# Routing logits of a mixture-of-experts layer: tokens stationary, gate weights moving

## The reference

```python
x = x + ffn(cond(x))                       # h = cond(x), [8192, 512]
logits = h @ gate_w.T                      # [8192, 64]
scores = softmax(logits, axis=-1)
topk_w, topk_i = top_k(scores, 6)          # the 6 experts of a token
# each expert takes its first 64 tokens: buf [64, 64, 512]
y = (silu(buf @ w_gate) * (buf @ w_up)) @ w_down
out = sum of y * topk_w, per token
shared = (silu(h @ sw_gate) * (h @ sw_up)) @ sw_down
```

## Time and profile before

| | us |
|---|---|
| median of three runs | 1214.61 |
| lowest and highest of the three | 1214.23, 1215.86 |
| the profiled execution | 1215.23 |
| its span, first to last instruction | 1213.4 |

### The profile page before, as it was taken

The page is one execution under the profiler, slowest core; times in us unless marked ns, Lnnn a source line. Parts: engine busy times, 40 slices in busy tenths (PEclk is TensorE's granted clock), DMA queues, the critical chain, the costliest instruction groups (busy, mean ns, idle before and its releaser), DMA issues.

```text
span 1213.4 us, 15977 instructions
## 1 busy us (share of the span) xinstructions
PE 1207.8 (100%) x5764; PEld 893.9 (74%) x5764; DVE 856.0 (71%) x1852; ACT 331.7 (27%) x630; POOL 269.7 (22%) x246
## 2 busy tenths in 40 slices
PE   9999999999999999999999999999999999999998
PEld 8888888888888888888866666666666666666666
DVE  6998989989889888886656556555655564655652
ACT  4544243433423443244111111120111201111111
POOL 0000000000000000000135355263453553553431
PEclk9999999999999999999999999999999999999999
DMA  9857445372543725245767988988989989999863
GB/s 200 211 137 195 96 122 130 83 172 67 165 106 84 184 73 153 61 135 189 249 218 248 334 267 274 349 273 277 342 235 335 314 280 305 295 306 301 275 147 84
DMA packets 159968, 250.92 MB, mean 207 GB/s; under 512 B 23633, under 2 KB 94673, under 8 KB 158737
## 3 DMA queue, kind: packets, MB, share of 16 engines
q1 hardware_dynamic: 143968, 223.53, 58.5%
q0 software_dynamic: 14048, 25.18, 10.5%
q10 hardware_dynamic: 1872, 1.18, 0.3%
HBM read 197.14 MB, written 61.10 MB: 213 GB/s over the span
## 4 chain that ended last, share of the span: by engine, by line
PE 93%; DVE 5%; issue 1%; ACT 0%; DMA 0%; POOL 0%; DVEq 0%; POOLq 0%; ACTq 0%
PE bank L1423 22%; PE bank L1424 22%; PE bank L1425 22%; PE bank L1625 13%; PE bank L1640 7%; PE bank L1456 2%; PE bank L1481 1%; PE bank L1544 1%; PE bank L1543 1%; PE bank L1479 1%; PE bank L1550 1%; PE bank L1492 1%; DVE hl L887 0%; DMA hg<-table,idx_quarter 0%; DVE x L902 0%
## 5 line engine op out<-in xcount | busy, mean ns | idle before, releaser
L1423 PE MATMUL bank<-hh,gu 128*128 128x512 f32 x704 | 278.0, 395 | 0.0
L1424 PE MATMUL bank<-hl,gu 128*128 128x512 f32 x704 | 274.2, 390 | 0.0
L1425 PE MATMUL bank<-hh,gu 128*128 128x512 f32 x704 | 274.1, 389 | 0.0
L600 POOL DMA_INDIRECT hg<-table,idx_quarter x128 | 124.7, 974 | 646.6 <-DVE idx_hi L1309 596.6
L1423 PEld LDWEIGHTS bank<-hh,gu 128*128 128x128 f32 x704 | 132.2, 188 | 39.1 <-issue 12.8
L1425 PEld LDWEIGHTS bank<-hh,gu 128*128 128x128 f32 x704 | 132.2, 188 | 27.9
L1424 PEld LDWEIGHTS bank<-hl,gu 128*128 128x128 f32 x704 | 132.3, 188 | 26.2
L668 ACT ACTIVATE ah<-prod 128x512 fp32r<-128x512 f32 x96 | 60.6, 632 | 302.0 <-DVE prod L969 295.9
L1382 DVE STREAM_TRANSPOSE eactT<-eact 32x96 f32<-32x96 f32 (+1 forms) x512 | 133.9, 262 | 7.9
L1423 PE MATMUL bank<-sdh,ah 128*128 128x512 f32 x320 | 126.0, 394 | 0.3 <-issue 0.3
L1424 PE MATMUL bank<-sdl,ah 128*128 128x512 f32 x320 | 124.6, 390 | 0.0
(11 more groups left out here) (126 smaller groups left out, 1676.0 us busy)
## 6 DMA issues: line engine op xcount, KB each, us to landing
wg<-in_L_ffn_w_gate_dram SPq DMA_DIRECT2D x64, 704.0 KB
wu<-in_L_ffn_w_up_dram SPq DMA_DIRECT2D x64, 704.0 KB
wd<-in_L_ffn_w_down_dram SPq DMA_DIRECT2D x64, 512.0 KB
table<-hrow SPq DMA_DIRECT2D x64, 256.0 KB, 4.3
x<-in_x_dram SPq DMA_DIRECT2D x60, 256.0 KB, 6.9
wd<-in_L_ffn_w_down_dram SPq DMA_DIRECT2D x64, 192.0 KB
out_dram<-outst SPq DMA_DIRECT2D x35, 256.0 KB
outst<-in_x_dram SPq DMA_DIRECT2D x32, 256.0 KB, 3.5
```

The lines of the kernel that those rows point to most:

```text
L600: nc.gpsimd.indirect_dma_start(out=hg[p % 3][:, b, :], out_offset=None, in_=quarters, in_offset=bass.IndirectOffsetOnAxis(ap=idx_quarter[: ...
L1423: nc.tensor.matmul(o, st_h, mv_h, start=first_mm, stop=False)
L1424: nc.tensor.matmul(o, st_h, mv_l, start=False, stop=False)
L1425: return nc.tensor.matmul(o, st_l, mv_h, start=False, stop=last_mm)
```

## The change

The logits of a chunk are computed in one step. `logits(n)` now takes the tokens as stationary operand: for each of four pieces of 128 tokens, 4 matmuls with a 128 x 128 piece of hh stationary and the 128 columns of gw2 moving, then 4 with a piece of hl stationary and only the 64 high columns of gw2 moving (the product of the low parts is left out). The result has tokens on partitions at once, in the bank from which `take_low` and `route` read before. `logits_raw`, `take_lraw`, the transposes, the buffer lsb (its bytes stay reserved, so no other buffer moves) and two semaphores go. The new `logits` stands where `logits_raw` stood; nothing stands any longer where the transposes stood. `take_low(b)` moves ahead of `silu(v, 0)` on ACT.

```diff
--- before.py
+++ after.py
@@ -114,7 +114,7 @@
         w3p = keep("w3p", [P, QC, D])
         qb = keep("qb", [P, 2 * B, KC])
         gw2 = keep("gw2", [P, KC, 2 * E], F32R)
-        lsb = keep("lsb", [P, CH])
+        keep.at += 4 * CH
         gu_end = keep.at
         hrow = keep("hrow", [P, CH // SQ, P])
         sc = keep("sc", [P, 2, J, E])
@@ -231,8 +231,6 @@
             hl_ready = sem("hl_ready")
             rows_taken = sem("rows_taken")
             rows_stored = sem("rows_stored")
-            lraw_filled = sem("lraw_filled")
-            lraw_taken = sem("lraw_taken")
             logits_filled = sem("logits_filled")
             llow_ready = sem("llow_ready")
             route_step = sem("route_step")
@@ -348,9 +346,6 @@
         def cond_bank(n, oc):
             return bank[(5, 6, 1, 2)[oc] if n == 0 else (3, 4, 5, 6)[oc] if n == 1 else (4, 5, 6, 4)[oc]]
 
-        def lraw_bank(n):
-            return bank[7 if n == 0 else 5]
-
         def logits_bank(n):
             return bank[7] if n == 0 else bank[3] if n % 2 == 0 else bank[6]
 
@@ -682,17 +677,12 @@
                 if n == 0 and oc == 0:
                     act.wait_ge(bias_loaded[1], 16 * (P // SQ))
                 if oc == 0:
-                    wait(act, s.lraw_filled, n)
+                    wait(act, s.logits_filled, n)
                     wait(act, s.gu_filled, GT * (n // 2))
                 nc.scalar.activation(h32[:, oc, :], cond_bank(n, oc)[:, :], ACT.Relu,
                                      bias=b2c[:, oc:oc + 1]).then_inc(s.cond_taken, 1)
                 act.wait_ge(s.cond_taken, KC * n + oc + 1)
                 copy(hh[:, oc, :], h32[:, oc, :]).then_inc(s.hh_ready, 1)
-
-            def take_lraw(n):
-                act.wait_ge(s.lraw_filled, n + 1)
-                wait(act, s.logits_filled, n)
-                copy(lsb[:, :], lraw_bank(n)[:, :]).then_inc(s.lraw_taken, 1)
 
             def take_low(n):
 
@@ -782,7 +772,6 @@
             split_xm(1, 1)
             split_piece(1)
             split_piece(2)
-            take_lraw(0)
 
             def body(i):
                 a, b, c, d = 2 * i, 2 * i + 1, 2 * i + 2, 2 * i + 3
@@ -796,7 +785,6 @@
                         silu_table()
                 if i == 0:
                     split_piece(3)
-                take_lraw(b)
                 if i == 0:
                     split_piece(4)
                     take_low(a)
@@ -804,9 +792,9 @@
                     split_piece(6)
                 if 0 < i < ND - 1:
                     split_xm(c, 0)
-                silu(v, 0)
                 if i > 0:
                     take_low(b)
+                silu(v, 0)
                 split_a(v, 0)
                 if not more:
                     take_ranks(i)
@@ -848,7 +836,6 @@
                     split_xm(d, 1)
                     if i < 2:
                         take_ranks(i)
-                    take_lraw(c)
 
             for i in range(ND):
                 body(i)
@@ -1429,8 +1416,6 @@
                     pe.wait_ge(s.xmh_ready, halves(n))
                     pe.wait_ge(s.xml_ready, halves(n))
                     pe.wait_ge(s.cond_taken, KC * n)
-                if oc == 1:
-                    pe.wait_ge(s.lraw_taken, n)
                 if oc == 2:
                     pe.wait_ge(s.z_ready, n if n % 2 == 0 else n - 1)
                 if oc == 3:
@@ -1469,28 +1454,27 @@
                 elif n == 1 and oc == KC - 1:
                     op.then_inc(s.cond_begun, 1)
 
-            def logits_raw(n):
-                pe.wait_ge(s.cond_taken, KC * n + 3)
+            def logits(n):
+
+                o = logits_bank(n)
                 if n == 0:
                     pe.wait_ge(s.gw2_ready, 2)
-                o = lraw_bank(n)
-                for k in range(KC):
-                    pe.wait_ge(s.hh_ready, KC * n + k + 1)
-                    nc.tensor.matmul(o[:, :], gw2[:, k, :], hh[:, k, :], start=(k == 0), stop=False)
-                    pe.wait_ge(s.hl_ready, KC * n + k + 1)
-                    op = nc.tensor.matmul(o[:, :], gw2[:, k, :], hl[:, k, :], start=False, stop=(k == KC - 1))
-                op.then_inc(s.lraw_filled, 1)
-
-            def logits(n):
-                pe.wait_ge(s.lraw_taken, n + 1)
-                if n > 0 and n % 2 == 0:
+                elif n % 2 == 0:
                     pe.wait_ge(s.z_ready, n - 1)
                     pe.wait_ge(s.cond_taken, 2 * KC)
-                elif n > 0:
+                else:
                     pe.wait_ge(s.cond_taken, KC * (n + 1))
                 for j in range(J):
-                    op = nc.tensor.transpose(logits_bank(n)[:, j * P:(j + 1) * P], lsb[:, j * P:(j + 1) * P],
-                                             ident[:, :])
+                    t = slice(j * P, (j + 1) * P)
+                    for k in range(KC):
+                        if j == 0:
+                            pe.wait_ge(s.hh_ready, KC * n + k + 1)
+                        nc.tensor.matmul(o[:, j * P:(j + 1) * P], hh[:, k, t], gw2[:, k, :], start=(k == 0), stop=False)
+                    for k in range(KC):
+                        if j == 0:
+                            pe.wait_ge(s.hl_ready, KC * n + k + 1)
+                        op = nc.tensor.matmul(o[:, j * P:j * P + E], hl[:, k, t], gw2[:, k, 0:E], start=False,
+                                              stop=(k == KC - 1))
                 op.then_inc(s.logits_filled, 1)
 
             def gu_tile(v, t):
@@ -1573,7 +1557,7 @@
             op.then_inc(s.gateT_filled, 1)
             for oc in range(KC):
                 cond_half(1, oc, 0)
-            logits_raw(0)
+            logits(0)
             for oc in range(KC):
                 cond_half(1, oc, 1)
 
@@ -1581,18 +1565,12 @@
                 a, b, c, d = 2 * i, 2 * i + 1, 2 * i + 2, 2 * i + 3
                 v, more = i, 2 * i + 2 < NCH
                 if i > 0:
-                    cond_tile(b, 0)
-                    logits(a)
-                    for oc in range(1, KC):
+                    for oc in range(KC):
                         cond_tile(b, oc)
                     down_tile(v - 1, 3)
-                else:
-                    logits(a)
-                logits_raw(b)
+                logits(b)
                 for t in range(GT):
                     gu_tile(v, t)
-                    if t == (2 if i == 0 else 0):
-                        logits(b)
                     if i > 0 and t == (5 if more else 2):
                         ranksT(i)
                 if more:
@@ -1601,7 +1579,7 @@
                     if i == 0:
                         ranksT(i)
                     down_tile(v, 0)
-                    logits_raw(c)
+                    logits(c)
                     down_tile(v, 1)
                     down_tile(v, 2)
```

## The result

| | us |
|---|---|
| before, median of 4 runs | 1214.42 |
| changed kernel, median of 4 runs (1240.01 to 1242.94) | 1241.32 |
| ratio, with its 95% interval | 1.0219 (1.0206 to 1.0232) |
| profiled execution, and its span | 1242.94, 1241.1 |

What follows compares the result with a forecast made beforehand. PE was taken to pace the kernel end to end. 1.86 + 2.22 + 1.02 + 18.5 gave +23.6 us; on the 1213.4 us span, plus 1.83, less 0.6 for the median: 1238 us, range 1223 to 1247.

Steps and rivals of the forecast that it cites:

- The pace: New logits matmuls on PE: 0.115 us between starts, 3.68 us a chunk against 2.26, +1.42 in each of 13 ordinary chunks.
- the uncovered load: Lower bound for a short matmul's distance: a float32r weight load not hidden under a stream, 0.108 us; sum then +20.0.
- The float32 matmuls: 13 earlier matmuls of 128 columns, taken as two passes, with 0.114 us between starts; the 0.115 was set next to them.
- several passes: Rival: float32r streams under 256 columns take four passes, 5.55 us a chunk, +53, 1268 us; chance 0.10.
- streams alone: Rival: all loads hidden, distances 0.067 and 0.041 us, 1.72 us a chunk, 1209 us; chance 0.04.
- loads that overlap: Rival: loads partly overlap each other, halfway distance 0.088 us, sum +9.9, 1224 us; chance 0.06.
- The rule on fast weight loads: Skill rule for 128 non-FP32 weights, in theory four times as fast; would hide the 32 loads; set aside for trace rows.
- Chunk 1: PE waits for the last hl tile and gets on 5.33 us after reaching the logits, before 2.67; net +2.22 us.
- Chunk 2: No wait for hl assumed at its logits, where there was one before: +1.02 us, up to +2.0 at the other end.
- Chunk 0: Its logits take 3.68 us in place of 1.816, with nothing credited for the removed transposes: +1.86 us.
- The edits at nothing: Moved waits on ACT, PSUM waits of `logits`, `take_low` ahead of `silu(v, 0)` and an earlier `route(b)`: counted as costing nothing.
- a falling clock: Lower granted clock during the bursts: said to look like four passes in the time; no size or chance of its own.

Runs made afterwards that it cites:

- the half loads: Changed kernel with 24 of a chunk's 32 weight loads at 64 columns, the other tokens' logits left incomplete; 1218.48 us (1.0025).
- the wider streams: Changed kernel with the 16 hl-stationary matmuls a chunk streaming all 128 columns of the gate weights, not 64; 1238.26 us (1.0192).
- the high parts alone: Changed kernel without the 16 hl-stationary matmuls a chunk, so 16 loads and streams and not 32; 1207.69 us (0.9947).
- the loops the other way round: Changed kernel with the same 32 matmuls a chunk, the four token pieces run inside each hh tile, then each hl tile; 1239.69 us (1.0211).
- the bursts of 8: Changed kernel with each chunk's 32 matmuls in bursts of 8 (16 at most) between wide tiles, chunk 1's wait filled with 8 wide matmuls; 1255.73 us (1.0343).
- two bursts: Changed kernel with each chunk's 32 matmuls, but for chunk 0's, as two bursts of 16 with a gate or down tile between; 1240.3 us (1.0209).
- two bursts and a filled wait: Changed kernel with chunks' 32 matmuls as two 16s, chunk 0's undivided, and 8 wide matmuls in PE's wait at chunk 1; 1238.55 us (1.0196).

## Why the prediction was right

It said 1238 us, 1223 to 1247; 1241.3 was measured. Point by point:

- **The pace.** 0.115 us for each of the 32 was 0.112: nearer to the lower bound, the uncovered load of the earlier trace rows, than to the 256-column matmuls of the earlier trace rows. The float32 matmuls of the earlier trace rows, at 0.114, were the right neighbour, but perhaps not for the reason given: that they take two passes stands in no row, and their own loads start 0.11 us apart in the trace too. An ordinary chunk pays 3.58 - 2.26 = 1.32 us, not 1.42; thirteen of them 17.2, not 18.5. That the load sets the pace was an argument from two rows; the half loads, the wider streams and the high parts alone show it. The same timelines put the rivals out: no distances of 0.23 and 0.12 (several passes), none of 0.07 and 0.04 throughout (streams alone), and no pace of 0.088 (loads that overlap).
- **The rule on fast weight loads.** The Trainium skill (TensorE: Matmul & The Clock Gate, Weight-path perf modes) gives a factor of four in theory for fp8 and no win for fp32; it doesn't name float32r. No run here shows a fast load for float32r: 0.112 us for 128 columns, 0.059 for 64. The prediction was right to keep its row, and the rule spoke less against it than it says there.
- **Chunk 1.** 5.33 us were worked out and 5.24 measured, where the clock held. One reading behind it was wrong: the PSUM waits of `logits` are not all for steps that ended long before, as at chunk 1 PE waits 0.78 us for ACT's h, ahead of the first short matmul. It cost nothing more only because the wait for hl ends later; with the loops the other way round it ends last. **Chunk 2** had no stall to speak of, 101.80 to 105.37 us, 0.08 more than chunk 4 from first start to the next step. **Chunk 0** took 3.67 us, as said, but what it replaces took 2.04 and not 1.82, for its first matmul was late before too: 0.2 us too much in the sum.
- **The edits at nothing** were that. Beside the one at chunk 1, no wait of PE grew in both traces of the changed kernel (the first has 0.8 us for ACT's w3p near the start, the second has not); the 0.4 us before the first expert went in both. `take_low` ahead of `silu(v, 0)` is harmless only because the logits are done before the gate tiles; the bursts of 8 show what it costs otherwise.
- **The step that failed** is the clock. The prediction named a falling clock in half a sentence, gave it no price and no chance of its own, and set it aside by a row of 68 transposes at 1.00. That row was no likeness: these are transposes, and a transpose's load is 49 ns shorter. Traces of the changed kernel lost 6.8 and 3.4 us to it (half of the falls), and executions of one variant at the full clock took 1236 to 1237. That the forecast missed by 3 us and not by 5 is luck: its loads were 1.7 us too dear (23.6 against 21.9 below), which hid a part of the clock's price.

With the terms as measured the sum is 1.6 + 2.1 + 1.0 + 17.2 = 21.9 us, against 22.2 and 22.3 in the two traces of two bursts, which have no fall. With 6.8 for the clock it is 28.7; the profiled execution was 28.4 longer up to the first expert (637.03 us against 608.64) and 0.7 shorter behind it. The clock's share of the 26.9 us in the median is some 3 to 5 us.

Three things stay open. What makes the clock fall: the runs show where it fell, and that neither a burst of 32 nor a wait ahead of one always does it. Why the falls outside chunk 1, four of four, came after odd chunks' bursts (7, 15, 5, 15) and never an even one's, when both kinds have the same 3.49 us from their first start to the next step. And what costs the kernel with two bursts and a filled wait 1 to 3 us in executions at a clock of 0.999 to 1.000; the part from the first expert on, which took 604.1 to 605.0 us in the traces, can hold up to 0.9 of it. No version here beats the kernel before but the one that drops the low part of h from the logits.

## What to carry to other kernels

Which operand is stationary is a price by the column: here a float32r column that streams costs PE 0.227/512 = 0.44 ns, one that is loaded 0.112/128 = 0.88 ns, and only the longer of the two counts. Tokens moving cost 8 x 512 x 0.44 ns and the transposes 0.44 us, 2.26 us a chunk; tokens stationary cost 32 x 128 x 0.88 ns, 3.58 us: a transpose that costs four short matmuls is cheap against 24 more loads. Ahead of making a moving operand narrow, look in the trace for an uncovered weight load (two starts on PEld, or a late matmul and the one behind it) and set that as the floor of each matmul.

## What the hardware showed that was not expected

PE's granted clock fell to 1.2 GHz while PE was busy throughout by the profile, right after 32 matmuls in a row that waited for their loads: in four places in three traces, for 3.3 to 3.4 us each, without a wait of PE ahead of them (0.50 in 202.40 to 205.70 us above). At chunk 1, with a wait of PE ahead, the clock fell within such a burst or right behind it, for 3.4 to 10.2 us, in each of the five traces that have both (one of them with half loads), though not in every execution. Right behind 16 in a row, in four traces, none; but some executions without a trace had a mean clock of 0.997 there too. A kernel can so lose clock while its matmuls are issued without a gap; the cause is not shown.
